# Token groups of 4 instead of 8 in the third layer's attention, a 128-row bias product, and gate rows spread by a transfer

## The reference

```python
qkv = x @ qkv_w + qkv_b
qkv = qkv.reshape(n, t, 3, H, DH)
q, k, v = (qkv[:, :, 0], qkv[:, :, 1], qkv[:, :, 2])
attn = jnp.einsum('nthd,ntkd->nthk', q * scale, k)
attn = jax.nn.softmax(attn, axis=-1)
out = jnp.einsum('nthk,ntkd->nthd', attn, v)
out = out.transpose(0, 2, 1, 3).reshape(n, t, d)
return out @ proj_w + proj_b
```

## Time and profile before

| | before |
|---|---|
| median of 3 runs | 2513.45 us (2508.41 to 2519.66) |
| the profiled execution | 2511.96 us, its span 2510.1 us |
| TensorE busy with matmuls | 2265.3 us, 90% of the span |
| VectorE busy | 1461.9 us, 58% |
| ScalarE busy | 1059.9 us, 42% |
| mean granted TensorE clock, share of 2.4 GHz | 0.893 |

### The profile page before, as it was taken

The page is one execution under the profiler, slowest core; times in us unless marked ns, Lnnn a source line. Parts: engine busy times, 40 slices in busy tenths (PEclk is TensorE's granted clock), DMA queues, the critical chain, the costliest instruction groups (busy, mean ns, idle before and its releaser), DMA issues.

```text
span 2510.1 us, 36691 instructions
## 1 busy us (share of the span) xinstructions
PE 2265.3 (90%) x14312; PEld 1661.8 (66%) x14312; DVE 1461.9 (58%) x2965; ACT 1059.9 (42%) x1677; POOL 509.5 (20%) x499
## 2 busy tenths in 40 slices
PE   7978998889889998989799998999999998899999
PEld 5343787558766885678365657788888755464648
DVE  4675268757774877487647653362435475755633
ACT  2534314352335234423526373443334263547463
POOL 3120034404420443143210101031210000200001
PEclk8676889899979988999989999797878899899999
DMA  5240322241223222322221304224040312021100
GB/s 156 73 126 21 102 64 73 59 122 53 80 64 95 63 65 63 103 79 65 85 72 33 92 18 59 64 56 98 21 94 16 106 33 80 28 84 60 47 11 20
DMA packets 199914, 169.69 MB, mean 68 GB/s; under 512 B 54098, under 2 KB 158842, under 8 KB 199738
## 3 DMA queue, kind: packets, MB, share of 16 engines
q1 hardware_dynamic: 193166, 154.64, 22.3%
q0 software_dynamic: 6576, 12.71, 1.8%
HBM read 126.09 MB, written 40.12 MB: 66 GB/s over the span
## 4 chain that ended last, share of the span: by engine, by line
PE 59%; DVE 25%; ACT 7%; issue 4%; DMA 2%; POOL 2%; SPq 1%; ACTq 0%; POOLq 0%; DVEq 0%
PE PSA L1803 12%; PE PSA L1818 11%; DVE MX L1459 7%; PE PSA L1709 6%; DVE FH L1350 4%; PE PSA L1599 4%; PE PSA L1686 4%; PE PSA L1699 4%; PE PSA L1656 4%; ACT PB L1298 4%; DVE HH L1578 3%; PE PSA L1727 2%; PE PSA L1738 2%; PE PSA L1622 2%; PE PSA L1668 2%
## 5 line engine op out<-in xcount | busy, mean ns | idle before, releaser
L1459 DVE TENSOR_REDUCE MX<-PSA 128x1 f32<-128x512 f32 x768 | 489.1, 682 | 282.9 <-PE PSA L1686 279.7
L1818 PE MATMUL PSA<-FH,HH 128*128 128x288 f32 x2016 | 470.9, 325 | 25.6 <-DVE HH L1578 25.6
L1803 PE MATMUL PSA<-A,FH 128*128 128x256 f32 x2520 | 453.5, 296 | 25.4 <-DVE FH L1350 20.3
L1334 ACT ACTIVATE HF<-PSA 128x512 f32<-128x512 f32 x252 | 150.2, 596 | 742.3 <-PE PSA L1803 597.4
L1298 ACT ACTIVATE PB<-PSA 128x1024 f32<-128x1024 f32 x384 | 371.3, 1027 | 140.1 <-PE PSA L1699 139.1
L1803 PEld LDWEIGHTS PSA<-A,FH 128*128 128x128 f32 x2520 | 373.2, 199 | 49.2 <-DVE FH L1350 29.4
L1818 PEld LDWEIGHTS PSA<-FH,HH 128*128 128x128 f32 x2016 | 332.8, 199 | 89.6 <-issue 45.2
L1207 POOL TENSOR_TENSOR X<-X,TM 128x288 f32<-128x288 f32 x176 | 155.5, 898 | 758.3 <-DVE TM L1523 758.3
L1818 PE MATMUL PSA<-FL,HH 128*128 128x288 f32 x1008 | 308.0, 306 | 0.0
L1202 POOL TENSOR_TENSOR FL<-ST,FH 128x544 fp32r<-128x544 f32 x171 | 247.6, 1449 | 261.5 <-DVE FH L1350 261.5
L1578 DVE TENSOR_TENSOR HH<-HF,HH 128x512 fp32r<-128x512 f32 x252 | 231.4, 918 | 109.0 <-ACT HH L1335 107.3
(11 more groups left out here) (161 smaller groups left out, 2744.3 us busy)
## 6 DMA issues: line engine op xcount, KB each, us to landing
qkd<-HH SPq DMA_DIRECT2D x48, 504.0 KB
ST<-in_L_cond_w SPq DMA_DIRECT2D x51, 432.0 KB
ST<-in_L_cond_w SPq DMA_DIRECT2D x102, 192.0 KB
QS<-qkd SPq DMA_DIRECT2D x88, 144.0 KB
KS<-qkd SPq DMA_DIRECT2D x88, 144.0 KB
QS<-qkd SPq DMA_DIRECT2D x144, 72.0 KB
KS<-qkd SPq DMA_DIRECT2D x144, 72.0 KB
ST<-in_L_cond_w SPq DMA_DIRECT2D x153, 48.0 KB
```

Of the source, the lines that this page charges most:

```text
L1334: e.activation(HF[f][:, :], PS[bk][:, :], gelu)
L1459: e.reduce_max(MX[p // 2 % 2][:, col:col + 1], PS[bk][:, :], axis=AX.X).then_inc(free[bk], 1)
L1803: m = e.matmul(PS[bk][:, s_ * 256:(s_ + 1) * 256], r(w_), r(x_[:, half * 256:(half + 1) * 256]), start=(z == 0), stop=(z == 6))
L1818: m = e.matmul(PS[bk][:, 0:C], r(HH[u][:, c, tk]), r(w_), start=False, stop=(j == NCH - 1 and z == 2))
```

## The change

1. Third layer: groups of 4 tokens. `cols` takes 64 columns with a step of 32 elements. Each product is 64 x 64, written to the lower or upper 64 partitions of a bank (`half`). A step of `s1b` is 32 products (two quarters x two halves x 8) into two banks, 4 steps for an item; a step of `s2b` covers all four quarters, 64 products into four banks, 2 steps for an item, and waits for the maxima of both pairs of quarters. `av2` takes 64 rows x 32 columns against 64 columns, 64 products a step into two banks, 2 steps for an item. In each of the three this is 256 pairs of load and matmul for an item. The number of banks to be reduced or exponentiated falls from 16 to 8 each. Mask rows fall from 8 to 4.
2. ON and B2 get 128 rows, zero but for the first two; the bias product runs over all 128.
3. `gates` becomes a transfer that SP issues, from the row of GR to all partitions of GB.
4. Order: the ring has all 8 banks in the third layer's attention stage; `mid` starts later there (`MID_AT`); `turn_x` of item i + 2 moves from the next attention stage to the end of `mid(i)`, after the last `fc1`; item 12's loads of queries and keys are no longer kept back (`at_end`, `ks1`).

```diff
-         "s1": 230, "s2": 450, "av": 230, "no": 500, "rows": 350, "qk2": 1650, "s1b": 900, "s2b": 900, "av2": 1400, "no2": 500, "rt": 3100}
+         "s1": 230, "s2": 450, "av": 230, "no": 500, "rows": 350, "qk2": 1650, "s1b": 1700, "s2b": 3000, "av2": 2500, "no2": 500, "rt": 3100}
-MID_AT = (0, 0, 4000)
+MID_AT = (8000, 14000)
+RING_A2 = (0, 1, 2, 3, 4, 5, 6, 7)
...
-    at_end = (0, 12)
+    at_end = (0,)
...
     def at2_steps(i):
+        exps = {}
+        for st in range(2):
+            bks = [ring() for _ in range(4)]
+            put("s2b", i, (0, 1, 2, 3), st, bks, (mrow[0], mrow[1]))
+            for qt in range(4):
+                put("s2b_exp", qt, st, bks[qt], pb_free[qt // 2])
+                exps[qt, st] = bks[qt]
+            yield
...
+        for u in range(2):
+            bks = (ring(), ring())
+            put("av2", i, u, bks, {k: v for k, v in exps.items() if k[0] // 2 == u}, vr[0])
...
+        if (i + 1) // 4 == 2:
+            while last_fc1[0] < i - 1:
+                yield
+            yield from turn_x(norm_of[i + 2], i % 2, (i + 2) // 4, 0, (i + 2) % 4)
+            turned_early.add(i + 2)
...
-            weave(ffn_steps(i - 1), ((m, MID_NS[kind], MID_AT[kind]), (side, S1_NS[kind], 0)))
+            weave(ffn_steps(i - 1), ((m, MID_NS[kind], MID_AT[i == 11] if L == 2 else 0), (side, S1_NS[kind], 0)))
...
-        B2 = [sb(f"B2{n}", [2, C]) for n in range(2)]
+        B2 = [sb(f"B2{n}", [128, C]) for n in range(2)]
-        ON = sb("ON", [2, 128])
+        ON = sb("ON", [128, 128])
...
         def cols(t_, i, qt, rows, j):
-            return view(t_[:, :, :], 32 * qt, i % 2 * H * 128 + j, [(1, rows, True), (16, 128, False)])
+            return view(t_[:, :, :], 32 * qt, i % 2 * H * 128 + j, [(1, rows, True), (32, 64, False)])
...
+                elif kind == "gates":
+                    i, g, gr, old = a
+                    w.wait_ge(free[gr[0]], gr[1] + 1)
+                    if old is not None:
+                        w.wait_ge(free[old[0]], old[1] + 1)
+                    e.dma_start(GB[:, g, :], view(GR[:, :, :], 32 * (i // 4 % 2) + i % 4, g * C,
+                                                  [(1, 1, True), (0, 128, False), (1, C, False)])).then_inc(s_gb[g], 16)
...
-                    i, u, z, bks, land = a
-                    w.wait_ge(s_qk[u], land)
+                    i, qts, st, bks, land = a
+                    w.wait_ge(s_qk[qts[0] // 2], land)
                     for bk, n in bks:
                         may_fill(bk, n)
-                    for c in range(4):
-                        for x, (bk, n) in enumerate(bks):
-                            m = e.matmul(PS[bk][:, c * 128:(c + 1) * 128], cols(QS, i, 2 * u + x, D + 8, 4 * z + c),
-                                         cols(KS, i, 2 * u + x, D + 8, 4 * z + c), start=True, stop=True)
+                    for c in range(8):
+                        for half in range(2):
+                            for qt, (bk, n) in zip(qts, bks):
+                                j = 16 * half + 8 * st + c
+                                m = e.matmul(PS[bk][64 * half:64 * half + 64, c * 64:(c + 1) * 64],
+                                             cols(QS, i, qt, D + 4, j), cols(KS, i, qt, D + 4, j), start=True, stop=True)
...
+                    for jj in range(16):
+                        x, y = jj // 4, jj % 4
+                        for sub in range(2):
+                            for half, (bk, n) in enumerate(bks):
+                                o = x * 128 + sub * 64
+                                m = e.matmul(PS[bk][32 * y:32 * y + 32, o:o + 64],
+                                             VF[64 * half:64 * half + 64, ((2 * u + sub) * 16 + jj) * V1:((2 * u + sub) * 16 + jj) * V1 + 32],
+                                             PB[u][64 * half:64 * half + 64, 2 * sub + jj // 8, jj % 8 * 64:(jj % 8 + 1) * 64],
+                                             start=True, stop=True)
...
-                elif kind == "gates":
-                    i, g, (bk, n), gr, _ = a
-                    L, b = i // 4, i % 4
-                    w.wait_ge(s_init, 6)
-                    w.wait_ge(free[gr[0]], gr[1] + 1)
-                    may_fill(bk, n)
-                    e.matmul(PS[bk][:, 0:C],
-                             view(ID[:, :], 32 * (L % 2), 32 * (L % 2) + b, [(1, 4, True), (0, 128, False)]),
-                             GR[32 * (L % 2):32 * (L % 2) + 4, g, :], start=True, stop=True).then_inc(full[bk], 1)
```

More of the change, by code:

```diff
@@ L707, in weave @@
                     last[n] = pe[0] + gap
+    last_fc1, turned_early = [-1], set()
     def pre(i):
-        yield from turn_x(norm_of[i], i % 2, i // 4, 0, i % 4)
+        if i not in turned_early:
+            yield from turn_x(norm_of[i], i % 2, i // 4, 0, i % 4)
         yield from proj_qk2(i) if i // 4 == 2 else proj_qk(i)
@@ L780, in plan @@
                 step_bg(2 if i == 0 else 1)
+                if i == 0 and not gb_ready[0] and (0, 0) in gr_ready:
+                    gates(0, 0)
                 if i == 0 and n == 8:
@@ L914, in build @@
         s_res = sem("residual_added")
+        s_gb = [sem(f"gate_rows{g}_landed") for g in range(2)]
         s_hh = sem("hidden_split")
@@ L1731, in pe_program @@
                 elif kind == "s2b":
-                    i, u, z, bks, land = a
-                    w.wait_ge(s_m[u], land)
+                    i, qts, st, bks, land = a
+                    w.wait_ge(s_m[0], land[0])
+                    w.wait_ge(s_m[1], land[1])
                     for bk, n in bks:
                         may_fill(bk, n)
-                    for c in range(4):
-                        for x, (bk, n) in enumerate(bks):
-                            m = e.matmul(PS[bk][:, c * 128:(c + 1) * 128], cols(KS, i, 2 * u + x, D + 9, 4 * z + c),
-                                         cols(QS, i, 2 * u + x, D + 9, 4 * z + c), start=True, stop=True)
-                            if c == 3:
-                                m.then_inc(full[bk], 1)
+                    for c in range(8):
+                        for half in range(2):
+                            for qt, (bk, n) in zip(qts, bks):
+                                j = 16 * half + 8 * st + c
+                                m = e.matmul(PS[bk][64 * half:64 * half + 64, c * 64:(c + 1) * 64],
+                                             cols(KS, i, qt, D + 5, j), cols(QS, i, qt, D + 5, j), start=True, stop=True)
+                                if c == 7 and half:
+                                    m.then_inc(full[bk], 1)
@@ L1753, in pe_program @@
-                    m.then_inc(full[bk], 1)
+                    for jj in range(16):
+                        x, y = jj // 4, jj % 4
+                        for sub in range(2):
+                            for half, (bk, n) in enumerate(bks):
[4 more added lines that the diff above has]
+                                             start=True, stop=True)
+                                if jj == 15 and sub:
+                                    m.then_inc(full[bk], 1)
```

165 lines of the change are left out of this document (72 added, 93 removed).

## The result

| | before | after |
|---|---|---|
| median | 2515.64 us (4 runs) | 2410.78 us (2400.34 to 2418.29, 4 runs) |
| ratio to before, 95% interval | | 0.9583 [0.954, 0.9627] |
| span of the profiled execution | 2510.1 us | 2398.6 us |

The change takes 105 us off; 2404 was predicted. First the page of the kernel after: busy time and share of the span, then what the DMA queues moved and which share of all 16 engines it took.

The account below looks back on a forecast made before the run. TensorE was taken as the bound (59% of the chain that ended last). From 2511.96 us: pace -66, bias -27, gates -16, clock -8, waits +12, boundaries -4 gave 2403, plus 1.5 for the median: 2404 us, range 2355 to 2480.

Parts of the forecast that it names:

- Pace: Third layer's s1b, s2b and av2 in groups of 4 tokens: 16.5 us less an item, 66 us for four.
- Reading A: Third layer's small products overlap across tiles in flight, so pairs get faster; the forecast with its sum, chance 0.60.
- The rule set against part 1: Third layer's small products: floor of about 25 ns between matmuls, or 62 ns with software decoding, giving 49.7 us an item.
- Clock: Third layer: shorter low-activity attention stage lets clock-bound work run faster, 2 us an item, 8 in all.
- New waits: Third layer: turns now wait behind the DVE and ACT chain, 3 us an item, 12 us added in all.
- Bias: Bias product over 128 rows: 0.40 us less each, 68 of 112 on the chain, 27 us less.
- Gates: Gate rows by transfer: 16 of 32 products and some ACT copies leave the chain, 16 us less.
- Boundaries: Item 8's mask-row wait, with mask transfers halved, and item 12's early loads: 4 us less.
- B: Third layer's small products: weight loads go in turn, so the token groups bring nothing; 2478 us, chance 0.20.
- The gain turns into waits: Latency chain lands in full behind each of four third-layer stages, 48 us instead of 12; 2440 us, chance 0.09.
- Slow pairs: Third layer's small row tiles cost 0.110 us a pair whatever the width; 2591 us, chance 0.07.
- a bias without effect: Bias product's cost is not the change of height, so 128 rows bring nothing; 2431 us, chance 0.04.

Follow-up runs that it names:

- e8: Kernel before, with queries and keys of s1b and s2b read 128 side by side instead of at a step of 16 elements; 2484.03 us, single run.
- e10: Kernel after, with 64 columns read two apart in items 9 and 11, side by side in 8 and 10, instead of 32 apart; 2396.21 us, single run.
- e1: Kernel after, unchanged, run again beside its variants; 2411.89 us, ratio 0.957.
- e6: Kernel after, with gate rows spread again by a TensorE product and an ACT copy instead of a transfer; 2412.14 us, ratio 0.9584.
- e5: Kernel after, with the bias product reading two rows again instead of 128; 2445.36 us, ratio 0.9711.
- e9: Kernel after, with the third layer's second gate transfer of an item issued ahead of the attention stage instead of inside it; 2408.22 us, ratio 0.9586.
- e12: Kernel after, with s1b going round four row quarters in a step, as s2b does; 2417.22 us, ratio 0.9605.
- e11: Kernel after, with the third layer's mid part starting 7 us later in the feed-forward schedule; 2420.1 us, ratio 0.9636.
- e2: Kernel after, with the attention-row stores queued ahead of the next item's stacking transfers on SP; 2409.27 us, ratio 0.9568.

## Why the prediction came out as it did

The number was 7 us off, its terms more so; their errors cancel. With the terms as measured the sum is 84 + 34 + 0 + 8 - 30 + 4 = 100 us, where 109 were forecast and 105 measured. That the time came so close is luck: 18 us too little for the pace stand against 18 too little for the waits.

- **Pace (66 predicted, 84 measured): right mechanism, size too small.** Reading A holds. e8 shows that the step between columns doubles the time of a pair, e10 the same at 64 columns, and the quarter of 0.110 for half the columns with twice the tiles came out as forecast (0.0275 taken, 0.027 measured; s1b 8.1 us an item predicted, 8.0 measured). Reading A's own sign of a matmul length near 270 ns was not met so well (288 and 306). What was mis-sized is the 0.025 "past the middle" for the steps with eight tiles in flight: s2b runs at (2.39 - 0.26)/128 = 0.017 and av2 at (1.73 - 0.26)/128 = 0.011. Both lie near the lower bounds of the prediction (0.014 and 0.008), the side of its own mechanism; the nearest row (0.032 of av2 before) had half the tiles and twice the columns. The sign named for A, s2b's group within 3.8 us, held with room.
- **The rule set against part 1.** No row shows 62 ns, and the 11 to 17 ns from start to start lie below the floor of about 25 ns that the Trainium skill states (TensorE: Matmul & The Clock Gate, "Back-to-back issue gap"). The same page of the Trainium skill has a load last its columns over 1.2 GHz ("LDWEIGHTS") and overlap other tiles only where the row group differs ("The mechanism"). That describes the contiguous reads of 128 columns at 2.4 GHz: an estimate from it is 107/2 = 53 ns in two quarters, 52 were measured (at 1.2 GHz 109). For 64 columns it would be 53/2 = 27 ns; the 13 measured fit only if the column halves overlap too, against the page. The prediction read it as agreeing with 110 ns in turn. That was a coincidence of the doubling by the step and the halving by two quarters.
- **Clock (8): about right.** The attention stages went from 0.67 to 0.70 up to 0.81 to 1.00, and the projections and modulation of the third layer take 11.7 us less (9.2 in e1). That this is all the clock gave is not separated by any run.
- **New waits (12): too small, 30 measured.** The chain behind XN was named and priced at 3 us an item; it is 3.8. The one behind POOL OT, 14.4 us, was missed. "Delaying mid by 8 us leaves its transfers more time" looked at the delay and not at the shorter attention stage, the SP queue in front of the stores and the gate transfer ahead of the q,k stores. Without gate transfers (e6) the layer idles 38.9 us, so 12 of the 30 belong to part 3, and the 12 were less far off than they look.
- **Bias (27): too small, about 34 by e5.** The price of one was nearly right (0.40 us less forecast, 0.17 + 0.19 = 0.36 measured; 0.13 forecast for one, 0.14 now to the next start). For 112 that is 40 us, less 19 of new idle time 21, no more than the count of 68 gives. The 12 us on top came with a lower clock in e5; whether the count of 68 or a term of clock that part 2 lacked was at fault stays open.
- **Gates (16): the step that failed; e6 gives nothing.** 144 KB were sized by a store of 288 KB (2.8 us); but a transfer that reads a single partition 128 times lands in 7.2 us and takes 4.0 us of the sixteen engines. (That the single partition is the reason was not tested by itself.) The 25.5 us that the products cost TensorE come back, but for 6, as 19 us of new idle time. That the transfer lengthens the wait behind POOL OT is shown by e6 and e9 (14.4 to 7.4 and 7.3 us), through the landing of the q,k stores and the stacking behind it. "Are not held", said of the transfers queued behind it in SP's queue, looked at SP's waits alone, not at what lands late.
- **Boundaries (4).** 5.0 to 1.3 us at item 8, as said.

The rivals: B as a whole is ruled out by e8 and e10. "The gain turns into waits" was right in kind, with some 30 us instead of 48. Slow pairs and a bias without effect did not occur. Open: why some 16 of the 25 us that the bias gives TensorE in layers 1 and 2 come back there as idle time behind VectorE's split of FH, where the 12 us of part 2 outside the rows lie, and what the 6.5 us before one step of e12 are.

## What to carry to other kernels

Ask of a small fp32 product how many tiles are in flight and whether its operands are read with a step, before counting columns: these two set the pace, and the second counts only at the high clock. When TensorE's part of a stage shrinks, lay the stage's chain of transfers against what is left of the work that hid it; moving the start (e11) or one transfer (e2, e9) just passes the wait on. A product replaced by a transfer is not free: price it by a row of the same pattern (one partition to all), not of the same size, and look at what lands behind it.

## What the runs showed of the hardware

- At 2.4 GHz pairs with fp32 operands read at a step of 16 or 32 elements take twice as long as contiguous ones in two row quarters (0.110 to 0.052 us, 0.027 to 0.013 a pair; 0.016 to 0.010 in four), those with a step of 2 do not; at 1.2 GHz stepped and contiguous pairs of 128 columns both cost 0.109 to 0.110.
- Pairs of load and matmul go at 15 to 17 ns in eight tiles of 64 columns with the step, at 10 ns without it, at 11 ns for 64 x 32 tiles without.
- Spreading one partition's 1152 bytes over 128 partitions by a transfer: 7.2 us to landing, 37 GB/s.
- A product of 2 rows between products of full height costs 0.17 us more itself than one of full height, and 0.19 us in the next one.
- Two profiled executions of one kernel (the kernel after and e1) differ by 19.5 us in 2400 at clocks of 0.913 and 0.902, their single waits and groups by 1 or 2 us.
